# Where two groups of weight splits, a reciprocal of row sums and a gate's inverse stand in the order of an attention layer's first two groups

## Chip, core and metric

The kernel runs on one core of one Trainium2 chip. The time is the device time of one launch in microseconds (us); the engines are TensorE (PE in the profile, its weight loads PEld), VectorE (DVE), ScalarE (ACT), GpSimd (POOL) and SyncE's queue of transfers (SPq).

## What is computed

The input x has 4 batches of 512 tokens with 1024 features. Each batch goes through one attention block and one gate:

```python
xn = layernorm(x)
q, k, v = xn @ Wq.T, xn @ Wk.T, xn @ Wv.T        # 32 query heads, 8 key/value heads of 128
q, k = rmsnorm(q) * q_norm_w, rmsnorm(k) * k_norm_w
attn = softmax(q k.T / sqrt(128) + slope[head] * (key - query), causal)
s = (attn @ v) @ Wo.T
g = silu(xn @ W.T + bias + lora(xn))
out = x + s * g
```

Everything is float32. A product of two float32 operands is made from three passes on TensorE: each operand is split into a high part (rounded to the type fp32r, on ScalarE) and a low part (the operand minus its high part, on GpSimd for weights, on VectorE for activations), and hi*hi, lo*hi and hi*lo are summed.

## The kernel before

**Groups, steps and products.** There are 32 groups n (4 batches times 8 key/value heads), each with 4 steps j (one query head each), so 128 steps m = 4n + j. A step computes scores, softmax and attention of one head, and beside it a part of the next group's projection. The projection of a group (queries, keys, values and gate columns: 896 columns) is done with a 2 by 2 block scheme with seven products P1 to P7 in place of eight. Each product needs a combination of blocks of the weights, so for each group and each half h of its rows the kernel makes four sums of weight blocks (`weight_sum` and `weight_sums`, the instructions at L1390, L1392, L1395 and L1398 on VectorE for the first groups, L1132, L1133, L1135 and L1137 on GpSimd from group 2 on). The products of group n+1 are made by step: j = 0 makes P1 and P2, j = 1 makes P6 and P7, j = 2 makes P4, j = 3 makes P5 and P3. There are four slots for halves of split weights (`wh`, `wl`), so splits run one product ahead of the matmuls.

**How weights come.** In the first batch each half of a group's weights passes through one place in SBUF (`xtok` from group 2 on): SyncE loads it (`load_weights` L327, `load_gate_weights` L336 and L338), stores three raw blocks (`store_halves` L347 and L348), GpSimd sums the blocks in place, SyncE stores the four sums (`store_sums` L355), and only when that store has landed does the load of the next half begin. The split weights are read back from DRAM (`load_w` L302, 448 KB for a half). The halves follow one another in this order: (1,0), (1,1), (2,0), (2,1), (3,0), (3,1) and so on, (group, half). (2,0) is loaded in step 0, stored and summed around step 1, (2,1) is loaded at the end of step 2 and summed in step 3, and (3,0) is loaded in step 4 and summed in step 5. The load of (2,0) waits for GpSimd's first low half of P7 (L445, `sp.wait_ge(w_ready, ...)`). Group 1's P1, P2, P6 and P7 aren't read back: `split_later` (L802) splits them from where the load has put them.

**Order on each queue.** Every engine runs its own program in the order that is written out in its `step(n, j)`; engines meet at semaphores only.

- ScalarE (L979 to L1052): the four exponentials of the step (`exps`, L879), the high part of the attention output before (`head_out`, L891), high parts of the turned keys or queries, the scaling of the probabilities by the inverse row sums (`normalise`, L886), the gate's input (j = 0) or the output weights' high part (`split_b`, L822, after a wait for their load), the squares for the norms, the high parts of the turned probabilities of key tiles 0 to 2 (`probs_hi`, L858), the split of the first product of the list (`split_product`, L788; by j: P6, P4, P3, P1), `probs_hi` of key tile 3, the split of the second product (P7, P5, none, P2).
- VectorE: the four score tiles with bias and row maximum (`score_max`, L1319), `row_sums_inverse` (L1325), the low part of the attention output (L1330), low parts of turned queries or keys (L1284), the norms' factors and scaled rows (L1262 to L1274), the additions of the products to `raw` (L1314), the gate, the additions to `acc` (L1342 and L1344), and the low parts of turned probabilities (`probs_lo`, L1284). In step 0 it also makes group 1's eight weight sums: the first ahead of the inverse of the row sums, the others after the low part of the queries.
- GpSimd: the bias of the next step (L1100), the low part of the output weights (L1092), the low part of v (j = 0, L1105), low parts of weights (L1074, L1081) and the weight sums. In group 0 the sums of (2,0) and (2,1) stand at the end of steps 1 and 3, behind the low parts of that step's second product (P5 and P2). From group 1 on they stand ahead of the low parts.
- TensorE: scores of the step with the attention products of the step before between them, turned queries or keys, the pieces of the products, two output projections, the transposes of the probabilities of key tiles 0 to 2, an output projection, the transpose of key tile 3, an output projection. Three banks take the transposes in turn, so the transpose of key tile 3 waits for `probs_lo` of key tile 0, and the next step's third score tile waits for the maximum of its first.

**The gate.** `gate_sum` (L1348) adds one, `gate_inverse` (L1354) takes four reciprocals of 128 columns each, `gate_product` (L1360) ends it in step j = 1. The inverses stand at the end of step j = 0, but in the last group of a batch (`late_gate`) they are spread over the four pieces of j = 1.

Of the kernel before, what the change touches and what calls it, by code (L numbers as in the profile page):

```python
# [34 lines left out]
P1, P2, P6, P7, P4, P5, P3 = range(NP)  # L35
# [29 lines left out]
def ln_group(b):  # L65

    return 6 if b == 1 else 5
# [48 lines left out]
def u_count(n, p, t):  # L116
    return HW * n + 2 * p + t + 1
# [10 lines left out]
def build_layer(nc, x_tok, x_first, xT, wa, wo, wT, lora_a, lora_bt, lw, ffn_b, qw, kw, rel, slopes,  # L128
                ident, outT):
    with ExitStack() as ctx:  # L130
# [114 lines left out]
        def prep_tile(g, h, a, c):  # L245

            at = 2 * a + c
            return prep_place(g, h)[:, at * 896:at * 896 + 896].rearrange("p (k n) -> p k n", k=2)
# [507 lines left out]
        def _(act):  # L756
# [33 lines left out]
            def split_later(p, h):  # L790

                w = LATER + 2 * p + h
                at = w - 4
                if p in (P1, P2):
                    act.wait_ge(prep_in[h], 192 * 2 - 64)
                else:
                    act.wait_ge(prep_t[h], 4 + 3)
                if h == 0:
                    act.wait_ge(w_half, at // 2 + 1)
                else:  # L800
                    act.wait_ge(u_done, u_count(0, at // 2, 1))
                act.activation(wh[:, w % 4], prep_tile(1, h, *QUARTER[p]), ACT.Copy).then_inc(w_hi_done, 1)  # L802
# [11 lines left out]
            def split_product(n, p):  # L814
                for h in range(2):
                    split_w(HW * n + 2 * p + h)
# [54 lines left out]
            def probs_hi(m, k):  # L871
                w = slice(PT_AT[k], PT_AT[k] + S - P * k)
                take_hi(("p", m, k), pT_hi[:, w], slice(P * k, S))
# [35 lines left out]
            def ln_scale(b, t):  # L909
                act.wait_ge(ln_newton, 5 * (b + 1))  # L910
                act.activation(xtok[:, t, :], xtok[:, t, :], ACT.Identity, bias=shift_x[:, t:t + 1],
                               scale=rinv_x[:, t:t + 1]).then_inc(ln_ready, 1)
# [59 lines left out]
            for t in range(2):  # L972
                square_rows(0, P3, t)
            rsqrt(0, 1)
            split_later(P1, 1)
            for h in range(2):
                split_later(P2, h)

            def step(n, j):  # L979
                b, g = divmod(n, HKV)  # L980
                m, v = 4 * n + j, 4 * n + j - 2
                exps(m)
                last = n + 1 == NG
                if m > 0:
                    head_out(m - 1)
                if last:
                    normalise(m)
                if j == 0:
                    queries_hi(n, 1)
                if j == 1:  # L990
                    queries_hi(n, 2)
                    queries_hi(n, 3)
                if j == 3 and not last:
                    keys_hi(n + 1)
                    queries_hi(n + 1, 0)
                if not last:
                    normalise(m)
                if j == 0:
                    gate_in(n)
                elif not last:  # L1000
                    split_b(v + 1)
                pieces, fills = unit_pieces(n, j), x_fills(n, j)
                for u in pieces:
                    if u[1] in (P1, P2):
                        take_piece(*u)
                    elif u[1] in (P4, P5, P3):
                        square_rows(*u)
                    if fills:
                        x_hi(fills.pop(0))
                    if (g, j) == (6, 3) and b == 0 and u[1] == P3:  # L1010
                        ln_scale(1, 2 + u[2])
                    if u[1:] == (P1, 1):
                        gate_exp_of(n)
                        split_b(v + 1)
                    if u[1:] == (P2, 0):
                        values_hi(n)
                if j == 0 and last:
                    gate_exp_of(n)
                    values_hi(n)
                if n + 1 < NG:  # L1020
                    if j == 0:
                        for t in range(2):
                            square_rows(n + 1, P2, t)
                    if j == 2:
                        rsqrt(n + 1, 0)
                    if j == 3:
                        rsqrt(n + 1, 1)
                while fills:
                    x_hi(fills.pop(0))
                if (g, j) == (6, 1) and 0 < b < BATCH - 1:  # L1030
                    for t in range(NT):
                        ln_scale(b + 1, t)
                for k in range(3):
                    probs_hi(m, k)
                if (g, j) == (ln_group(b + 1), 1) and b + 1 < BATCH:
                    ln_rsqrt(b + 1)
                if (g, j) == (6, 2) and b == 0:
                    ln_scale(1, 0)
                    ln_scale(1, 1)
                if m == 0:  # L1040
                    for h in range(2):
                        split_later(P6, h)
                else:
                    split_product(*[(n + 1, P6), (n + 1, P4), (n + 1, P3), (n + 2, P1)][j])
                if last:
                    split_b(v + 1)
                probs_hi(m, 3)
                if m == 0:
                    for h in range(2):
                        split_later(P7, h)  # L1050
                elif j != 2:
                    split_product(*[(n + 1, P7), (n + 1, P5), None, (n + 2, P2)][j])  # L1052

            for n in range(NG):
                for j in range(G):
# [162 lines left out]
        def _(dve):  # L1218
# [178 lines left out]
                    dve.wait_ge(prep_t[h], 4 * g + 3)  # L1397
                    dve.tensor_tensor(b21, b21, b22, ALU.subtract).then_inc(prep_t[h], 1)  # L1398

            def weight_sums(g, h):  # L1400
                for p in (P5, P7, P6, P4):
                    weight_sum(g, h, p)

            def low_first_half(p, h):
                w = 2 * p + h
                dve.wait_ge(w_hi_done, w + 1)
# [75 lines left out]
            def step(n, j):  # L1482
                b, g = divmod(n, HKV)
                m, v = 4 * n + j, 4 * n + j - 2
                more, next_x = n + 1 < NG, b + 1 < BATCH
# [6 lines left out]
                    scale_rows("q0")  # L1492
                score_max(m, 2)
                score_max(m, 3)
                if n == 0 and j == 0:
                    weight_sum(1, 0, P5)
                row_sums_inverse(m)
                if m > 0:
                    head_out(m - 1)
                if j == 0 and more:  # L1500
                    queries_lo(n, 1)
                    if n == 0:
                        weight_sum(1, 0, P7)
                        weight_sum(1, 0, P6)
                if j == 1 and more:
                    queries_lo(n, 2)
                    queries_lo(n, 3)
# [3 lines left out]
                if j == 0:  # L1511
                    row_factors(n, 1)
                    scale_rows("q2")
                    scale_rows("q3")
                    if n == 0:
                        weight_sum(1, 0, P4)
                        weight_sums(1, 1)
                if not more:
                    last_part(n, j)
                    return  # L1520
                late_gate = g == 7 and next_x
                pieces, fills = unit_pieces(n, j), x_fills(n, j)
                turned = []
                for i, u in enumerate(pieces):
                    p, t = u[1:]
# [127 lines left out]
```

## Time and profile before

| | us |
|---|---|
| median of 3 runs | 2654.61 (2654.4 to 2656.84) |
| the profiled execution, its own time | 2655.72 |
| its span | 2653.9 |
| TensorE busy | 2583.1 (97%) |
| VectorE, ScalarE, GpSimd busy | 1699.8, 1764.6, 1718.0 |
| mean granted TensorE clock | 0.995 of full speed |

The span is the stretch from the first to the last instruction. Busy time is the time in which an engine has an instruction running; for TensorE ends are modelled, so that two matmuls that follow each other overlap a little in the rows. A row of the timeline gives the start, the duration, the engine, the line of the kernel, the operation and the tiles, and in brackets how long the engine had been idle before it and whose result it had waited for.

### The profile page before, as it was taken

To read this page: it belongs to the slowest core of one execution; us is meant where nothing else is said; L and a number is where in the kernel's file an instruction comes from. 1 tells how busy PE (TensorE), PEld (TensorE's weight loads), DVE (VectorE), ACT (ScalarE), POOL (GpSimd) and SP (SyncE) were. 2 spreads that over 40 slices of the span, in tenths; PEclk is the share of its full clock that TensorE was granted. 3 is DMA by queue.
4 is the path that set the end of the run, shared out by engine and by line. 5 is a ranking of instruction groups with operands and counts; after the bars stand their busy time and mean duration, and the time that the engine had idled before them with its cause. 6 is when DMAs were issued, how large, how long until landed. Compare 5 with 4: busy or idle time off the path is not lost.

```text
span 2653.9 us, 39893 instructions
## 1 busy us (share of the span) xinstructions
PE 2583.1 (97%) x13840; PEld 2288.9 (86%) x13840; DVE 1699.8 (64%) x3533; ACT 1764.6 (66%) x4633; POOL 1718.0 (65%) x839
## 2 busy tenths in 40 slices
PE   6789999999999999999999999999999999999997
PEld 5778888888888888888888888888888888888886
DVE  7565656666766665666667666666666756656656
ACT  4565666767767666667766667666777666667764
POOL 3577887785767565655667756565666766656555
PEclk9899999999999999999999999999999999999999
DMA  7868878875354333433344433433334533333323
GB/s 283 289 219 278 265 261 272 271 258 166 118 171 154 113 106 118 140 112 118 106 137 155 128 119 111 144 106 118 109 104 137 189 106 108 115 116 112 112 78 131
DMA packets 171896, 414.78 MB, mean 156 GB/s; under 512 B 31024, under 2 KB 63920, under 8 KB 170800
## 3 DMA queue, kind: packets, MB, share of 16 engines
q1 hardware_dynamic: 170144, 410.19, 47.1%
q8 instruction: 112, 1.84, 0.3%
q10 hardware_dynamic: 1552, 2.04, 0.2%
q14 instruction: 88, 0.72, 0.1%
HBM read 339.81 MB, written 89.13 MB: 162 GB/s over the span
## 4 chain that ended last, share of the span: by engine, by line
PE 90%; DVE 3%; DMA 2%; POOL 2%; ACT 1%; SPq 1%; issue 0%; ACTq 0%; POOLq 0%; DVEq 0%
PE proj L508 21%; PE proj L510 21%; PE proj L509 21%; PE tr L608 5%; PE tr L588 3%; PE sc L508 3%; PE sc L509 3%; PE sc L510 3%; PE ot L509 3%; PE ot L510 3%; PE ot L508 3%; DMA wu<-xtok 1%; PE tr L581 1%; DMA wl<-wu 1%; POOL wl L1081 1%
## 5 line engine op out<-in xcount | busy, mean ns | idle before, releaser
L1081 POOL TENSOR_TENSOR wl<-wl,wh 128x896 fp32r<-128x896 f32 x428 | 909.1, 2156 | 552.3 <-ACT wh L788 552.2
L508 PE MATMUL proj<-wh,xh 128*128 128x448 f32 x1792 | 670.7, 374 | 7.3 <-ACT raw L827 2.2
L509 PE MATMUL proj<-wl,xh 128*128 128x448 f32 x1792 | 657.9, 367 | 0.0
L510 PE MATMUL proj<-wh,xl 128*128 128x448 f32 x1792 | 657.8, 367 | 0.0
L1092 POOL TENSOR_TENSOR wb_lo<-wb_lo,wb_hi 128x1024 fp32r<-128x1024 f32 x128 | 307.7, 2404 | 303.7 <-ACT wb_hi L822 303.7
L879 ACT ACTIVATE misc<-misc,negmax 128x128 f32<-128x128 f32 (+3 forms) x512 | 286.7, 565 | 266.3 <-DVE negmax L1319 266.1
L508 PE MATMUL proj<-o_hi,wb_hi 128*128 128x512 f32 x1024 | 425.2, 415 | 7.4 <-DVE acc L1344 3.5
L1344 DVE TENSOR_TENSOR acc<-acc,proj 128x512 f32<-128x512 f32 x476 | 324.8, 683 | 149.7 <-PE proj L510 147.8
L858 ACT ACTIVATE pT_hi<-tr 128x512 fp32r<-128x512 f32 (+3 forms) x512 | 197.5, 440 | 325.9 <-PE tr L608 325.9
L510 PE MATMUL proj<-o_hi,wb_lo 128*128 128x512 f32 x1024 | 403.6, 394 | 0.0
L509 PE MATMUL proj<-o_lo,wb_hi 128*128 128x512 f32 x1024 | 401.3, 392 | 0.0
L788 ACT ACTIVATE wh<-wl 128x896 fp32r<-128x896 f32 x428 | 387.9, 965 | 19.7 <-DMA wl<-wu 19.2
L1314 DVE TENSOR_TENSOR raw<-raw,proj 128x448 f32<-128x448 f32 x320 | 197.4, 617 | 301.9 <-PE proj L510 300.1
L508 PEld LDWEIGHTS proj<-wh,xh 128*128 128x128 f32 x1792 | 337.9, 189 | 37.1 <-ACT raw L827 4.9
L510 PEld LDWEIGHTS proj<-wh,xl 128*128 128x128 f32 x1792 | 337.4, 188 | 30.0
L509 PEld LDWEIGHTS proj<-wl,xh 128*128 128x128 f32 x1792 | 338.1, 189 | 27.8
L1319 DVE CUSTOM_DVE_ANT_0 misc<-sc,misc 128x128 f32<-128x128 f32 (+3 forms) x512 | 240.9, 487 | 175.9 <-PE sc L510 174.7
L1284 DVE TENSOR_TENSOR pT_lo<-tr,pT_hi 128x512 fp32r<-128x512 f32 (+3 forms) x512 | 226.6, 484 | 74.7 <-ACT pT_hi L858 74.4
L834 ACT ACTIVATE junk<-raw 128x128 f32<-128x128 f32 x640 | 189.8, 301 | 97.2 <-DVE raw L1314 93.4
L886 ACT ACTIVATE misc<-misc,rs_inv 128x128 f32<-128x128 f32 (+3 forms) x512 | 245.2, 558 | 1.0 <-DVE rs_inv L1325 1.0
L508 PEld LDWEIGHTS proj<-o_hi,wb_hi 128*128 128x128 f32 x1024 | 193.4, 189 | 51.7 <-DVE acc L1344 4.1
L1100 POOL TENSOR_SCALAR misc<-misc,slope 128x512 f32<-128x512 f32 x128 | 233.6, 1825 | 4.1 <-DMA misc<-rel 4.1
(135 smaller groups left out, 4438.1 us busy)
## 6 DMA issues: line engine op xcount, KB each, us to landing
wl<-wu SPq DMA_DIRECT2D x426, 448.0 KB, 3.9
wb_lo<-wo_in SPq DMA_DIRECT2D x128, 512.0 KB, 3.3
wu<-xtok SPq DMA_DIRECT2D x13, 1792.0 KB, 9.7
wo_in<-wo SPq DMA_DIRECT2D x32, 512.0 KB, 6.2
xtok<-wa SPq DMA_DIRECT2D x52, 256.0 KB, 4.0
wu<-xtok SPq DMA_DIRECT2D x13, 896.0 KB, 6.2
gate_dram<-misc SPq DMA_DIRECT2D x32, 256.0 KB, 5.0
xtok<-xT SPq DMA_DIRECT2D x28, 256.0 KB, 5.1
```

Of the source, the lines that this page charges most:

```text
L508: pe.matmul(out, hi_l, hi_r, start=first, stop=False, skip_group_check=onto)
L509: pe.matmul(out, hi_l, lo_r, start=False, stop=False, skip_group_check=onto)
L510: return pe.matmul(out, lo_l, hi_r, start=False, stop=last, skip_group_check=onto)
L788: act.activation(w_slot(wh, w), w_slot(wl, w, True), ACT.Copy).then_inc(w_hi_done, 1)
L879: act.activation(p, p, ACT.Exp, bias=negmax[:, i:i + 1], scale=-1.0, accum_out=rowsum[:, i:i + 1]).then_inc(exp_done, 1)
L886: ins = act.activation(p, p, ACT.Copy, scale=rs_inv[:, i:i + 1])
L1081: pool.tensor_tensor(w_slot(wl, w), w_slot(wl, w, True), w_slot(wh, w), ALU.subtract).then_inc(w_ready, 1)
L1092: pool.tensor_tensor(wb_lo[:, v % 2, :], wb_lo[:, v % 2, :].bitcast(F32), wb_hi[:, v % 2, :], ALU.subtract).then_inc(wb_ready, 1)
L1100: pool.tensor_scalar(bias_sb[:, m % 2, :], rel_sb[:], slope[:, m % H:m % H + 1], None, ALU.mult).then_inc(bias_ready, 1)
L1284: dve.tensor_tensor(dst, bank, hi, ALU.subtract).then_inc(tr_free, 1)
L1319: dve.tensor_tensor_reduce(prob[:, P_AT[i]:P_AT[i] + w], sc_ps[i % 2][:, 0:w], bias_sb[:, m % 2, S - w:S], -1.0, 3e38, ALU.add, ALU.min, n ...
L1344: dve.tensor_tensor(a, a, bank, ALU.add).then_inc(out_free, 1)
```

## The change

On ScalarE the rest of group 1's early splits (P1's second half and P2) goes from ahead of step 0 to behind its exponentials. In steps 1, 3, 4 and 5 the split of the second product is taken out of its place at the end of the step and stands behind the exponentials of the next step, ahead of `head_out`. In the first two groups `probs_hi` of key tile 3 stands directly behind those of key tiles 0 to 2, ahead of the first product's split. On VectorE the inverse of step 0's row sums has no weight sum ahead of it any more, six of group 1's eight weight sums stand together behind the low part of the queries, and the last two behind the scaled rows. The gate's inverses of group 0 move from the end of step 0 to step 1. GpSimd's and SyncE's programs aren't changed.

```diff
@@ scalar, before and in step(n, j)
             rsqrt(0, 1)
-            split_later(P1, 1)
-            for h in range(2):
-                split_later(P2, h)
+
+            def second(n, j):
+
+                split_product(*[(n + 1, P7), (n + 1, P5), None, (n + 2, P2)][j])
+
+            def deferred(n, j):
+
+                return 0 < 4 * n + j < 6 and j != 2
 
             def step(n, j):
...
                 exps(m)
                 last = n + 1 == NG
+                if m == 0:
+                    split_later(P1, 1)
+                    for h in range(2):
+                        split_later(P2, h)
+                elif deferred(*divmod(m - 1, 4)):
+                    second(*divmod(m - 1, 4))
                 if m > 0:
                     head_out(m - 1)
...
+                if n < 2:
+                    probs_hi(m, 3)
                 if m == 0:
                     for h in range(2):
                         split_later(P6, h)
...
-                probs_hi(m, 3)
+                if n >= 2:
+                    probs_hi(m, 3)
                 if m == 0:
                     for h in range(2):
                         split_later(P7, h)
-                elif j != 2:
-                    split_product(*[(n + 1, P7), (n + 1, P5), None, (n + 2, P2)][j])
+                elif j != 2 and not deferred(n, j):
+                    second(n, j)
@@ vector, step(n, j)
                 score_max(m, 3)
-                if n == 0 and j == 0:
-                    weight_sum(1, 0, P5)
                 row_sums_inverse(m)
                 if m > 0:
                     head_out(m - 1)
                 if j == 0 and more:
                     queries_lo(n, 1)
                     if n == 0:
-                        weight_sum(1, 0, P7)
-                        weight_sum(1, 0, P6)
+                        for h in range(2):
+                            for p in (P5, P7, P6):
+                                weight_sum(1, h, p)
...
                     if n == 0:
-                        weight_sum(1, 0, P4)
-                        weight_sums(1, 1)
+                        for h in range(2):
+                            weight_sum(1, h, P4)
...
-                late_gate = g == 7 and next_x
+                late_gate = g == 7 and next_x or n == 0
```

## Rows read from the trace of the kernel before

**Rows 1.** Page, part 1: busy time, share of the span, instructions by engine.

```profile
PE 2583.1 (97%) x13840; PEld 2288.9 (86%) x13840; DVE 1699.8 (64%) x3533; ACT 1764.6 (66%) x4633; POOL 1718.0 (65%) x839
```

**Rows 2.** Waits of TensorE, 86 to 420 us: for whom, total us, times, longest.

```profile
PE tr L608 <- DVE pT_lo L1284: 11.3, 4, 6.0
PE sc L508 <- DVE negmax L1319: 6.2, 4, 2.8
...
PE proj L508 <- DVE acc L1344: 1.5, 1, 1.5
```

**Rows 3.** Two stretches: busy time of each engine, granted clock, transfers' share, GB/s.

```profile
112.00:116.00 4.00, 2.21 (x9) 2.12 (x10) 3.38 (x9) 1.70 (x3) 3.79 (x3) 0.50 1.02 417
...
330.00:400.00 70.00, 70.00 (x372) 62.25 (x371) 41.88 (x86) 48.46 (x130) 57.70 (x28) 1.00 0.80 266
```

**Rows 4.** Timeline of TensorE, steps 0 to 6: start, us, what, idle before and releaser.

```profile
113.79 0.48 PE L608 MATMUL tr<-ident_sb,misc 128*128 128x128 f32 x1 [6.02 <-DVE pT_lo L1284]
...
135.21 0.44 PE L508 MATMUL sc<-kT_hi,qT_hi 128*128 128x384 f32 x1 [0.74 <-DVE negmax L1319]
...
152.98 0.47 PE L608 MATMUL tr<-ident_sb,misc 128*128 128x128 f32 x1 [3.59 <-DVE pT_lo L1284]
...
180.09 0.44 PE L508 MATMUL sc<-kT_hi,qT_hi 128*128 128x384 f32 x1 [1.07 <-DVE negmax L1319]
...
206.37 0.44 PE L508 MATMUL sc<-kT_hi,qT_hi 128*128 128x384 f32 x1 [2.81 <-DVE negmax L1319]
...
233.81 0.47 PE L508 MATMUL proj<-wh,xh 128*128 128x448 f32 x1 [0.53 <-POOL wl L1081]
```

**Rows 5.** Timeline of VectorE, steps 0 and 4.

```profile
94.14 2.85 DVE L1390 TENSOR_TENSOR xtok<-xtok 128x896 f32<-128x896 f32 x1 [3.98 <-DMA wu<-xtok]
...
109.80 3.39 DVE L1354 RECIPROCAL misc<-misc 128x128 f32<-128x128 f32 x4
113.11 1.80 DVE L1284 TENSOR_TENSOR pT_lo<-tr,pT_hi 128x512 fp32r<-128x512 f32 x4
...
182.66 0.69 DVE L1319 CUSTOM_DVE_ANT_0 misc<-sc,misc 128x512 f32<-128x512 f32 x1 [1.01 <-PE sc L510]
```

**Rows 6.** Timeline of ScalarE, steps 0, 1, 3 and 4.

```profile
114.30 0.28 ACT L858 ACTIVATE pT_hi<-tr 128x128 fp32r<-128x128 f32 x1 [2.38 <-PE tr L608]
...
129.25 1.06 ACT L822 ACTIVATE wb_hi<-wb_lo 128x1024 fp32r<-128x1024 f32 x1 [4.56 <-DMA wb_lo<-wo_in]
...
181.69 0.95 ACT L788 ACTIVATE wh<-wl 128x896 fp32r<-128x896 f32 x1 [1.09 <-DMA wl<-wu]
...
184.03 0.70 ACT L879 ACTIVATE misc<-misc,negmax 128x512 f32<-128x512 f32 x1
```

**Rows 7.** Timeline of GpSimd, steps 0 and 5.

```profile
111.15 2.08 POOL L1074 TENSOR_TENSOR wl<-xtok,wh 128x896 fp32r<-128x896 f32 x1 [3.87 <-ACT wh L802]
...
115.50 2.11 POOL L1074 TENSOR_TENSOR wl<-xtok,wh 128x896 fp32r<-128x896 f32 x1 [0.21 <-ACT wh L802]
...
220.77 2.13 POOL L1132 TENSOR_TENSOR xtok<-xtok 128x896 f32<-128x896 f32 x1 [1.88 <-DMA wu<-xtok]
```

**Rows 8.** Timeline of SyncE's queue, steps 0 and 1.

```profile
104.17 0.37 SPq L355 DMA_DIRECT2D wu<-xtok  x1
...
109.46 0.37 SPq L355 DMA_DIRECT2D wu<-acc  x1
117.69 3.96 SPq L327 DMA_DIRECT2D xtok<-wa  x8
```

**Rows 9.** The chain of waits, 130 to 234 us: start, us, what held it.

```profile
151.60 5.95 DMA wu<-xtok
...
178.83 6.26 POOL wl L1081 x3
185.09 2.10 POOL xtok L1132
...
194.12 6.84 DMA wu<-xtok
...
229.57 4.20 POOL wl L1081 x2
```

More of the change, by code:

```diff
@@ L1398, in weight_sum @@
                     dve.tensor_tensor(b21, b21, b22, ALU.subtract).then_inc(prep_t[h], 1)
-            def weight_sums(g, h):
-                for p in (P5, P7, P6, P4):
-                    weight_sum(g, h, p)
             def low_first_half(p, h):
```

## The prediction

> **What bounds the kernel.** I began with the busy times: TensorE has 97% of the span [rows 1], so only what gives TensorE a wait, or takes one away, can move the end. Next I asked whom TensorE waits for from the start of step 0 on. The waits that the change can touch are behind the low parts of probabilities, the row maxima and the output additions, some 19 us in nine waits [rows 2]. A later stretch shows TensorE busy for 70.00 of 70.00 us at full clock [rows 3], so past step 7 nothing that another engine does earlier is worth anything. All that can be won lies in steps 0 to 6, and a lead or a delay that TensorE has at the end of step 6 is carried to the end of the kernel unchanged. The waits stand in order in [rows 4]. After a long wait the granted clock is at its lower level: in the 4 us that hold the wait of 6.02 it was 0.50 [rows 3], 1.2 instead of 2.4 GHz, though TensorE had run at 2.4 before it idled.
>
> The last view is the chain of waits [rows 9]. It says that the small waits hang on one ring: load a half's weights, store them, sum them on GpSimd, store the sums (151.60 and 194.12), load the next half. It ends in step 6, where GpSimd makes both low parts of P4 from 229.57 on, right behind the sums of (3,0), and TensorE takes up the second half at 233.81 [rows 4]. So at 233.81 the ring, not TensorE, sets the time. That is the point on which I settle the sum.
>
> **Step 0.** VectorE's work from 94.14 to 113.11 is nearly unbroken: the sums, with the inverse of the row sums between them, then the gate's four reciprocals, 109.80 to 113.11 [rows 5]. The order of the sums costs nothing in itself, since they are all still there; the inverse of the row sums comes some 6 us earlier, ScalarE scales the probabilities before TensorE needs them, and TensorE's P2 pieces start about 2 us earlier. But the transpose of key tile 3 waits for VectorE. Without the reciprocals `probs_lo` starts at 109.8, and the transpose runs at 110.4 instead of 113.79 [rows 4]: 3.4 us won. The idle time before it stays near 6 us, because what TensorE did earlier it also ends earlier; the slow clock stays.
>
> The reciprocals go to step 1, one behind each piece: 3.39 / 4 = 0.85 us each [rows 5]. A piece's 12 matmuls last some 2.3 us at 70.00 / 372 = 0.19 us from start to start [rows 3], more than an addition and a reciprocal, so three are hidden; the fourth would hold `probs_lo` back by 0.4 us, and that is covered by ScalarE's wait below. Cost nothing; without that cover 0.4.
>
> **What that does to the ring.** ScalarE used to split P6 at once and take key tile 3 at 114.30 [rows 6]. Now key tile 3 comes first, at 110.9, and P6's splits behind it. The first takes 0.95 us (the duration of a split, [rows 6]), so GpSimd starts P6 at 112.05 instead of 111.15 [rows 7]. Its low half takes 2.1 us, three of them end P7's first half at 118.35, against 115.50 + 2.11 = 117.6. SyncE waits for exactly that before it loads (2,0), at 117.69 [rows 8]: the ring starts 0.7 us late. The high part of the output weights waits for a load behind it on the same queue (4.56 us of waiting, until 129.25 [rows 6]), and now until 129.95. ScalarE has that wait ahead of the high parts of step 1's probabilities. Of TensorE's 3.4 us some 0.3 are left at the end of step 1.
>
> A second thing happens in the queue. Group 1's last sums now stand side by side, so the store of (1,0), issued at 104.17, goes out at about 108.3, and the store of (1,1) at about 109.5 as before [rows 8]. Its cost for the load at 118.4 is bounded by 0 (both landed) and by one more store less the gap, worked out under the second rival as 2.6. I take 0.3 of it, nearer the lower end, since the load's eight parts are issued over 3.96 us [rows 8] and a backlog shrinks meanwhile.
>
> **Steps 2 and 3.** Key tile 3's high part no longer stands behind a split: the wait of 0.74 goes. P5's split, which waited for its load ahead of the exponentials, now waits behind them; the attention output and the squares come up to 2 us earlier, and the wait of 3.59 starts and ends with them [rows 4]. TensorE is about 1.9 us ahead at the start of step 3. There ScalarE waits for the next output weights, whose load hangs on the ring (from 151.60 on, [rows 9]) and comes 0.4 to 1.0 later. The lead shrinks to between 0.3 and 0.9; I take 0.5.
>
> **Step 4, where the ring loses.** The wait of 1.07 goes [rows 4]. The last score's maximum was taken at 182.66 and took 0.69 [rows 5]; now it is ready at 183.35 - 1.07 - 0.5 = 181.8. The last exponential takes 0.70 [rows 6] and ends at 182.5. Before, P2's second half was split at 181.69, when its load had come, ahead of the exponentials [rows 6]. Now both halves of P2 stand behind them. GpSimd can take up the first at 182.5 + 0.95 = 183.45, and needs 2 x 2.1 us. Behind them on its queue stand the sums of (2,1), which used to start at 185.09, right when P1's and P2's last three low parts ended (178.83 + 6.26, [rows 9]). Now they start at 187.7: **2.6 us later**. That is the price of the deferral, and it is paid on the ring: the store goes out at 196.7 instead of 194.12, its landing frees the place for (3,0) [rows 9], and the sums of (3,0), which waited 1.88 us for their data at 220.77 [rows 7], start at 223.4.
>
> **Steps 5 and 6.** The wait of 2.81 and its slow clock go [rows 4], because key tile 3 is no longer behind P6's splits. TensorE then waits some 2 us for the low parts of P6 and P7, whose loads are 2.6 late. It is at P4 at about 230, near 2 us early. But P4's low halves end at 229.57 + 2.1 + 2.6 = 234.3 and 236.4. Idle for over 4 us, TensorE comes back at 1.2 GHz, as after 6.02 [rows 3, 4]. The first half's six matmuls fill the 2.1 us until the second is there even so; if another 1.3 us are slow, they cost 0.7. The bounds for the clock are 0 (no fall, as after 0.53) and 2 (half of a 4 us stretch). The other deferred splits (P7 in step 5, P5 in step 6) are covered: GpSimd is still at P6 and at the sums when they come.
>
> **Sum.** 2.6 for the ring and 0.7 for the clock, less nothing: all that steps 0 to 5 win is waited away at P4. 2655.7 + 3.3 = 2659.0 for the profiled execution. It lies 1.1 above the median, so 2657.9 for the median. With the lead into step 4 between 0.3 and 0.9 and the clock between 0 and 2 the likeliest case alone spans 2656.8 to 2659.8.
>
> **Rivals.**
> - *The ring doesn't lose.* If the exponentials of step 4 end by 181.7, P2's splits are bound by their load, as before, and GpSimd's sums start on time. That needs a lead of 1.3 us into step 4. Then the ring is 0 to 1 late, and P4 comes when it came before: 2654.6 to 2656. For it: the lead was 1.9 a step before. Against it: the output weights' load in step 3. Chance 0.22.
> - *Stacked stores, slower.* The two stores of group 1 go out 1.2 us apart. One store of four sums takes 5.95 to 6.84 us to land [rows 9]. If the second moves only behind the first, it lands at 109.5 + 2 x 5.95 = 121.4, and the load issued at 118.4 moves about 2.6 us later than it could. Then the ring is 3.3 late from the start, TensorE is 2.1 late instead of 0.5 early in step 4, and the sums of (2,1) start 5.2 late; with the clock's 0.7 that is 5.9, 2660.5. It decides once the load of (2,0) is held over 2 us. Against it: the eight parts of the load are paced by their issue. Chance 0.13. The Trainium skill, "DMA: Bandwidth & Descriptors", section "Queues, rings and completion order", says that on each transfer engine descriptors are consumed in ring order, which speaks for this rival; by that rule the time would be 2660.5, and no row here shows two such stores side by side.
> - *The ring has slack that I don't see, faster.* If ScalarE's waits for loads in steps 1 and 3 moved with TensorE, the 3.4 of step 0, 0.74, 1.07 and 2.81 + 1.7 of clock would all count: 9.7 us, 2644.9. Against it: rows 9 show the ring without a gap. Chance 0.10.
> - The change does what it says: each moved instruction has its place in the diff, and no wait is taken off a semaphore.
>
> **Numbers.** The forecast has 0.55. A measurement of this kernel tells 0.2%, 5.3 us, from no change, that is 2649.3 and 2659.9. Faster: the last rival, 0.10. Slower: the second rival, 0.13, and 0.05 of the forecast's upper end. Same: 0.72. The range takes in the forecast, the first rival and the second, and reaches down part of the way to the last: 2651.5 to 2661.
>
> **What would show it.** Right: no wait of 2.81 before step 5's third score; the reciprocals in step 1; SyncE's first load of (2,0) near 118.4; the sums of (2,1) starting near 187.7 behind P2's low parts; the sums of (3,0) near 223.4; TensorE waiting some 4 us for `wl` in step 6, at 1.2 GHz behind it, and no difference in pace past 250 us. Wrong: the sums of (2,1) at 185 or before, or TensorE waiting in step 6 for something else than GpSimd.

## The result and the profile after

The changed kernel takes 2660.02 us (median of 15 runs, 2655.92 to 2663.26), the kernel before 2654.68 in the same sittings. The ratio is 1.0020, with a 95% interval of 1.0011 to 1.0028: **slower by 5.3 us**, clear of the scatter and right at the 0.2% that the prediction took as its bound (2659.9). One of the 15 runs of the kernel before took 3630.14 us, where the others took 2652.71 to 2656.84, and isn't in the ratio. The forecast was 2657.9 with a range of 2651.5 to 2661.

The profiled execution took 2660.54 us, its span is 2658.7 (4.8 more than before). Step 0 begins 0.9 us earlier in this trace than in that of before (its third score tile starts at 86.21 in place of 87.12); that lies in the start of the run, ahead of anything the change touches. Shifts of places in the trace are therefore told below as read and, in brackets, with those 0.9 us taken out.

The waits of TensorE in the changed kernel, 86 to 420 us (for whom, total us, times, longest), against [rows 2]:

```profile
PE tr L608 <- DVE pT_lo L1298: 13.2, 4, 4.9
PE proj L508 <- DVE acc L1358: 4.4, 1, 4.4
...
PE tr L588 <- DVE raw L1288: 2.7, 2, 1.8
PE sc L508 <- DVE negmax L1333: 2.3, 2, 1.6
```

The waits for the row maxima fell from 6.2 to 2.3 us, as they were meant to. Those for the low parts of probabilities grew from 11.3 to 13.2, and two others that had been short are long: the one for an addition to `acc` grew from 1.5 to 4.4, those for scaled rows from 0.4 to 2.7.

The same places as [rows 4] in TensorE's timeline:

```profile
108.70 0.48 PE L608 MATMUL tr<-ident_sb,misc 128*128 128x128 f32 x1 [4.90 <-DVE pT_lo L1298]
...
150.61 0.33 PE L608 MATMUL tr<-ident_sb,misc 128*128 128x128 f32 x1 [3.77 <-DVE pT_lo L1298]
...
160.24 0.65 PE L588 MATMUL tr<-ident_sb,raw 128*128 128x128 f32 x4 [1.83 <-DVE raw L1288]
...
202.96 0.80 PE L508 MATMUL proj<-o_hi,wb_hi 128*128 128x512 f32 x1 [4.43 <-DVE acc L1358]
...
237.17 0.47 PE L508 MATMUL proj<-wh,xh 128*128 128x448 f32 x1 [0.53 <-POOL wl L1095]
```

Key tile 3 of step 0 is turned at 108.70 instead of 113.79 (4.2 us earlier without the start). The waits of 0.74, 1.07 and 2.81 are gone. TensorE waits in step 3 (1.83 at 160.24, where it had waited 0.35) and in step 4 (4.43 at 202.96, where it had waited 1.48) instead, and takes up the second half of P4 at 237.17 instead of 233.81, 3.4 us late (4.3).

Two stretches of the changed kernel (busy time of each engine, granted clock, transfers' share, GB/s), against [rows 3]:

```profile
160.00:164.00 4.00, 3.76 (x14) 3.44 (x15) 2.81 (x9) 3.31 (x9) 1.61 (x1) 0.65 0.93 270
...
204.00:208.00 4.00, 4.00 (x11) 3.06 (x10) 1.78 (x5) 1.21 (x3) 0.67 (x1) 0.50 0.87 316
...
330.00:400.00 70.00, 70.00 (x377) 62.42 (x376) 43.78 (x92) 46.55 (x121) 57.78 (x29) 1.00 0.80 263
```

Behind both longer waits the granted clock is at its lower level, 1.2 GHz, for part or all of 4 us, though it had been 1.00, 2.4 GHz, from 156 to 160 and from 196 to 200. From 330 to 400 us TensorE is busy throughout at full clock, as before.

GpSimd around the sums, against [rows 7] and [rows 9]:

```profile
178.81 4.21 POOL L1095 TENSOR_TENSOR wl<-wl,wh 128x896 fp32r<-128x896 f32 x2 [6.01 <-ACT wh L788]
185.09 4.19 POOL L1095 TENSOR_TENSOR wl<-wl,wh 128x896 fp32r<-128x896 f32 x2 [2.07 <-ACT wh L788]
189.24 2.12 POOL L1146 TENSOR_TENSOR xtok<-xtok 128x896 f32<-128x896 f32 x1
...
224.15 2.12 POOL L1146 TENSOR_TENSOR xtok<-xtok 128x896 f32<-128x896 f32 x1 [1.01 <-DMA wu<-xtok]
...
232.91 4.20 POOL L1095 TENSOR_TENSOR wl<-wl,wh 128x896 fp32r<-128x896 f32 x2
```

Here is the ring. GpSimd stands idle for 2.07 us between the low parts of P1 and P2, since ScalarE's split of P2 is behind the exponentials of step 4, and the sums of (2,1) start at 189.24 in place of 185.09, those of (3,0) at 224.15 in place of 220.77, the low parts of P4 at 232.91 in place of 229.57.

The chain of waits of the changed kernel, where [rows 9] had gone over the sums:

```profile
183.36 0.82 ACT misc L879 x2
184.18 0.27 ACT wh L788
...
184.92 0.94 ACT wh L788
185.86 0.49 ACT o_hi L891
186.37 0.69 DVE o_lo L1344
...
193.51 5.10 DVE raw L1288 x2
...
202.36 0.55 DVE acc L1358
202.96 0.80 PE proj L508
```

From P2's split (`wh`) it doesn't go on to GpSimd's low parts and sums, but over the attention output, VectorE's scaled rows and the gate to the addition that TensorE waits for in step 4. So P2's split delays two paths, this one and the ring. They meet in step 6: P4's first low part is ready at 235.01, TensorE takes it up at 235.19, and the second half waits for GpSimd.

### The profile page after: what moved, and what is told of

Read it like the earlier page. It is cut to its first block, busy times and chain, and to the rows that moved or that the text cites. A ratio compares the mean times of both kernels' runs of the same rounds, so it can differ in the third digit from the quotient of the medians.

```text
span 2658.7 us, 39893 instructions
## 1 busy us (share of the span) xinstructions
PE 2584.6 (97%) x13840; PEld 2290.3 (86%) x13840; DVE 1706.4 (64%) x3533; ACT 1764.2 (66%) x4633; POOL 1716.2 (65%) x839
## 3 DMA queue, kind: packets, MB, share of 16 engines
q10 hardware_dynamic: 1552, 2.04, 0.2%
## 4 chain that ended last, share of the span: by engine, by line
PE 89%; DVE 4%; ACT 2%; POOL 2%; DMA 1%; issue 1%; SPq 1%; ACTq 0%; POOLq 0%; DVEq 0%
PE proj L508 21%; PE proj L510 21%; PE proj L509 21%; PE tr L608 5%; PE tr L588 3%; PE sc L508 3%; PE sc L509 3%; PE sc L510 3%; PE ot L509 3%; PE ot L510 3%; PE ot L508 3%; PE tr L581 1%; DVE raw L1288 0%; DMA wl<-wu 0%; DVE wl L1417 0%
```

## The experiments

Twelve kernels ran. Every ratio is against the kernel before in the same runs; 0.001 is 2.65 us.

The expectations name three explanations. *Ring theory*: the time is set by the ring of load, store, sums, store and next load, and a change costs what it delays there. *VectorE theory*: TensorE is held up in steps 3 and 4 by VectorE, whose scaling runs beside GpSimd's instructions. *Slack theory*: the ring has time to spare, and TensorE's own waits are what counts.

### One part at a time: which engine's edits cost?

ScalarE's edits alone. Against the changed kernel, all of VectorE's edits are undone:

```diff
                 score_max(m, 3)
+                if n == 0 and j == 0:
+                    weight_sum(1, 0, P5)
                 row_sums_inverse(m)
...
-                        for h in range(2):
-                            for p in (P5, P7, P6):
-                                weight_sum(1, h, p)
+                        weight_sum(1, 0, P7)
+                        weight_sum(1, 0, P6)
...
-                        for h in range(2):
-                            weight_sum(1, h, P4)
+                        weight_sum(1, 0, P4)
+                        weight_sums(1, 1)
...
-                late_gate = g == 7 and next_x or n == 0
+                late_gate = g == 7 and next_x
```

> Only ScalarE's edits of the change; VectorE's program is the one of before. Ring theory: the loss is ScalarE's, so it is here whole: 2659 to 2661, and the 3.4 us of step 0 aren't even won. VectorE theory: steps 3 and 4 run as in the changed kernel whenever ScalarE's step 2 ends early, so 2658 to 2661 too; the two differ by the next run.

2663.88 us, ratio 1.0033 (1.0020 to 1.0045): 9 us slower than before, 4 slower than the whole change.

VectorE's edits alone. They are the part of the change's diff that stands above under "vector"; ScalarE's program is the one of before, so no split is put off and key tile 3 stands where it stood. Its last line:

```diff
-                late_gate = g == 7 and next_x
+                late_gate = g == 7 and next_x or n == 0
```

> Only VectorE's edits; ScalarE's program is the one of before. Ring theory: the transpose of key tile 3 in step 0 comes 3.4 us earlier, P6's splits aren't held back by it, the ring starts no later than before, and nothing puts P2's split off: 2653 to 2655, no difference or up to 2 faster. VectorE theory: a lead into step 3 only lengthens the blocked scaling, 2654 to 2656. A loss of over 3 us here would say that it comes from the gate's inverse or the bunched stores.

2654.30 us, ratio 0.9998 (0.9989 to 1.0007): no difference. TensorE's transpose of key tile 3 in step 0 is earlier, at 111.91, and nothing comes of it.

So the loss is ScalarE's, VectorE's edits take back 4 us of it and give nothing by themselves. The two effects don't add, as the ring theory says of step 0: with VectorE late, key tile 3 (turned at 115.30 in the first of these runs) holds back P6's splits and with them the load of (2,0), which is issued at 123.34 there and at 116.74 in the changed kernel. The first run lies 3 us above what was expected of it: I hadn't counted that VectorE's edits are what makes the early key tile 3 bearable.

### The single part that the prediction blamed

P2's split of group 2, alone, on the kernel before:

```diff
                 exps(m)
+                if m == 4:
+                    split_product(2, P2)
...
-                elif j != 2:
+                elif j != 2 and m != 3:
                     split_product(*[(n + 1, P7), (n + 1, P5), None, (n + 2, P2)][j])
```

> The kernel before, with one single part of the change: P2 of group 2 is split behind step 4's exponentials. Ring theory: key tile 3's high part of step 3 isn't moved, so step 4 starts as before with its wait of 1.07, the exponentials end near 183.5 to 184, P2's low parts come 3 to 4 us later than before, and so do the sums of (2,1); the time is 2657 to 2659. Rival, many small parts: since putting P2 back in the full change won only 0.7 us, P2's place is worth under 1 us here too, 2654.5 to 2655.5.

2658.92 us, ratio 1.0015 (1.0007 to 1.0024): 4.4 us slower, as much as most of the change. GpSimd's timeline of this kernel:

```profile
174.80 4.28 POOL L1083 TENSOR_TENSOR wl<-wl,wh 128x896 fp32r<-128x896 f32 x2 [4.14 <-ACT wh L788]
183.27 4.20 POOL L1083 TENSOR_TENSOR wl<-wl,wh 128x896 fp32r<-128x896 f32 x2 [4.19 <-ACT wh L788]
187.42 2.13 POOL L1134 TENSOR_TENSOR xtok<-xtok 128x896 f32<-128x896 f32 x1
```

One moved split makes a hole of 4.19 us in front of P2's low parts and the sums. It also lengthens the wait of TensorE in step 4 from 1.5 us to the same 4.4 as in the changed kernel:

```profile
PE tr L608 <- DVE pT_lo L1286: 12.8, 4, 7.6
PE sc L508 <- DVE negmax L1321: 4.4, 5, 1.5
PE proj L508 <- DVE acc L1346: 4.4, 1, 4.4
```

The split pushes the attention output and the queries' high part back on ScalarE, VectorE starts its factors and scaled rows later and does them beside GpSimd's sums, and the addition that TensorE waits for comes behind all of it. In the trace of before the first of the small instructions for the factors took 0.66 us and the two scalings 3.23, here they take 1.75 and 5.09. So P2's place costs on two ways at once, the ring and step 4 itself. The chain of waits goes over the ring in this run and over step 4 in the changed kernel; no run takes one of the two away and leaves the other.

### Putting parts back into the change

P2 of step 3 back at the end of its step:

```diff
-                return 0 < 4 * n + j < 6 and j != 2
+                return 0 < 4 * n + j < 6 and j not in (2, 3)
```

> The changed kernel, but the second half of the splits that step 3 puts off (P2 of group 2) stands at the end of step 3 again. Ring theory: the sums of (2,1) start right behind P2's low parts, which come when their load has landed (183 plus two low parts), near 186 in place of 189.2, the sums of (3,0) 3 us earlier than in the changed kernel, and 2.5 to 4 us of the loss come back: 2656 to 2657.5. Rival, VectorE theory: VectorE, held up by GpSimd in steps 3 and 4, is what TensorE waits for (1.83 and 4.43 us); then the split's place is worth under 1 us: 2659 to 2660.5.

2659.37 us, ratio 1.0014 (1.0005 to 1.0023). The profiled execution does what the ring theory says, the sums of (2,1) start at 186.13 and those of (3,0) at 221.01, and it took 2657.48 us; but the median over 11 runs is 0.7 us below the change's only (1.6 by the two ratios, whose intervals overlap). The expectation of 2.5 to 4 us failed. TensorE comes to P4 ahead of GpSimd in this trace and waits 2.04 us for the first low part, which it doesn't in the changed kernel.

No split put off at all:

```diff
-                return 0 < 4 * n + j < 6 and j != 2
+                return False
```

> The changed kernel with no split put off at all, only the early high part of key tile 3 and VectorE's edits left. Ring theory: as with P2 alone put back, 2656 to 2657.5, since the other splits that are put off are covered, but with up to 2 us more, because P5's and P6's neighbours hold the exponentials back again (0.7 at step 2, 2 at step 5). VectorE theory: 2659 to 2661.

2657.75 us, ratio 1.0011 (1.0002 to 1.0020): 2.3 us below the change, 2.9 above before. VectorE's edits alone took 2654.30, so what is left of ScalarE's edits here, the early key tile 3 and group 1's first splits, costs 3.4 us by the medians, though the two intervals overlap. The splits put off aren't the whole loss.

Key tile 3 of step 0 behind P6's splits again:

```diff
-                if n < 2:
+                if n < 2 and m > 0:
                     probs_hi(m, 3)
...
-                if n >= 2:
+                if n >= 2 or m == 0:
                     probs_hi(m, 3)
```

> The changed kernel, with key tile 3's high part of step 0 behind P6's splits again (one place of eight). Ring theory, first part: P6's low parts start about 2 us earlier, the load of (2,0) comes 0.7 to 2 us earlier after the start of step 0, and 0.5 to 2 us come back: 2658 to 2659.5. Rival: the ring's start has slack or is given back by step 2, since P5's split waits for the exponentials: 2660.

2659.56 us, ratio 1.0021 (1.0012 to 1.0029): nothing, alone.

Both put back:

```diff
-                return 0 < 4 * n + j < 6 and j != 2
+                return 0 < 4 * n + j < 6 and j not in (2, 3)
...
-                if n < 2:
+                if n < 2 and m > 0:
                     probs_hi(m, 3)
```

> Both places that the ring theory holds responsible are put back: P2's split of step 3 and key tile 3 of step 0. Everything else of the change stays. Ring theory: the sums of (2,1) and of (3,0) start no later than before, and the time is that of before or up to 2 us below it, 2652.5 to 2655. VectorE theory: steps 3 and 4 still wait for VectorE, 2657 to 2659.

2656.86 us, ratio 1.0008 (0.9999 to 1.0017): 3.2 us below the change. It lies between what the ring theory expected (up to 2655) and what the VectorE theory did (from 2657). Each alone gave 0.5 to 0.7, both together 3.2, and 2.3 are left, at the edge of what the runs tell from nothing. That the two help only together fits one ring with two places where it is held up, but no run shows why the first alone gives so little; with medians that differ by less than their intervals this stays open. In this trace, too, TensorE is at P4 too early:

```profile
231.46 0.44 PE L508 MATMUL proj<-wh,xh 128*128 128x448 f32 x1 [2.02 <-POOL wl L1095]
```

### Is it VectorE beside GpSimd?

The wait of 1.83 in step 3 was in no step of the prediction. VectorE's scaling of two rows takes 5.05 us there. The run holds GpSimd's low parts of P3 back until it is done:

```diff
                 else:
+                    if m == 2:
+                        pool.wait_ge(q_ready, 5)
                     low_product(*[(n + 1, P6), (n + 1, P4), (n + 1, P3), (n + 2, P1)][j])
```

> The changed kernel, with one wait added on GpSimd: in step 2 it begins P3's low parts only when VectorE has scaled the first queries of the next group in step 3. VectorE theory: the two scalings of step 3 took 5.05 us because GpSimd's low parts ran beside them; without that they take 1.3 to 1.6, TensorE's wait of 1.83 goes and step 3 ends 2 to 3 us earlier; if that is what makes the loss, 2657 to 2658. Ring theory: the ring's next sums of (2,1) start only with P2's low parts behind step 4's exponentials, so they come earlier by what step 4 starts earlier, up to 2.5 us, and the time falls by as much, 2657.5 to 2659; with the sums no earlier, no time is won.

2659.19 us, ratio 1.0018 (1.0009 to 1.0027). VectorE's timeline at that place, in the changed kernel:

```profile
155.13 5.05 DVE L1288 SCALAR_TENSOR_TENSOR raw<-raw,tmp 128x512 f32<-128x512 f32 x2
```

and in this one, the same two instructions:

```profile
157.05 1.29 DVE L1290 SCALAR_TENSOR_TENSOR raw<-raw,tmp 128x512 f32<-128x512 f32 x2
```

Both are as expected of contention: 5.05 us beside GpSimd, 1.29 without. TensorE's wait of 1.83 and the slow clock behind it are gone, step 3 lasts 22.1 us (155.21 to 177.32) instead of 25.6 (153.17 to 178.81). But step 3 also begins 2.0 us later, so 1.5 of the 3.5 us are left at the start of step 4. The sums of (2,1) start 1.5 us earlier than in the changed kernel (187.77), those of (3,0) 1.6, and the span is 1.7 shorter; the median falls by 0.8, to 0.2 above the ring theory's range. P2 stands where it stood, and the wait of 4.43 in step 4 is in this trace too. VectorE's hold-up in step 3 is real and makes at most a small part of the loss. The same hold-up in step 4, where the scalings take 5.09 us here too, no run takes away.

### Moving the ring by itself

The strongest test leaves ScalarE as before and moves only GpSimd's sums (VectorE has its edits, which cost and bring nothing):

```diff
                 else:
+                    if m == 3:
+                        weight_sums(2, 1, (0,))        # the first two sums
                     low_product(*[(n + 1, P6), (n + 1, P4), (n + 1, P3), (n + 2, P1)][j])
+                if m == 1:
+                    weight_sums(2, 0)
...
-                if j in (1, 3) and n == 0:
-                    weight_sums(2, j // 2)
+                if m == 3:
+                    weight_sums(2, 1, (1,))            # the last two sums
```

> ScalarE as before, VectorE's edits of the change, and GpSimd reordered: the sums of (2,0) ahead of P5's low parts, and the first two sums of (2,1) ahead of P1's. The ring is made earlier where the change made it later. Ring theory: the store of (2,0)'s sums goes out 4 us earlier, that of (2,1) 3 to 5 us earlier, TensorE's waits in steps 5 and 6 (2.8, its slow clock 1.7, and 0.5) go, 2648 to 2651. If the ring isn't what sets the time, no difference, 2654 to 2656.

**2648.42 us, ratio 0.9978 (0.9969 to 0.9987): 6.2 us faster than before and 11.6 faster than the change.** It beats both kernels. Its GpSimd timeline:

```profile
136.68 2.10 POOL L1133 TENSOR_TENSOR xtok<-xtok 128x896 f32<-128x896 f32 x1
...
170.09 2.12 POOL L1133 TENSOR_TENSOR xtok<-xtok 128x896 f32<-128x896 f32 x1 [1.05 <-DMA wu<-xtok]
172.17 2.12 POOL L1134 TENSOR_TENSOR xtok<-xtok 128x896 f32<-128x896 f32 x1
174.90 8.38 POOL L1081 TENSOR_TENSOR wl<-wl,wh 128x896 fp32r<-128x896 f32 x4 [0.61 <-ACT wh L788]
183.23 2.13 POOL L1138 TENSOR_TENSOR xtok<-xtok 128x896 f32<-128x896 f32 x1
```

The sums of (2,0) start at 136.68 (before: 143.11, ahead of P5's low parts now), two sums of (2,1) fill time in which GpSimd had been idle, and the last two end at 187.6, 6.5 us before their end before. Of TensorE's waits the 1.5 us for an addition to `acc` in step 4 are gone, and none for a row maximum is longer than 1.8 us (2.8 before):

```profile
PE tr L608 <- DVE pT_lo L1291: 10.9, 4, 6.8
PE sc L508 <- DVE negmax L1326: 5.7, 4, 1.8
```

Then the same GpSimd order under the full change:

> The full change, with GpSimd's sums early as in the run that beat both kernels. Ring theory: the last two sums of (2,1) still stand behind P2's low parts, which the change puts off, so the loss against the kernel with early sums stays: 5 to 8 us above it, 2653 to 2656; against the change alone 4 to 6 us come back. Rival, slack: with the ring early the change's earlier exponentials count, and it is as good as the kernel with early sums, 2646 to 2649.

2655.75 us, ratio 1.0001 (0.9992 to 1.0010). The change costs 7.3 us more than the same order without it. The first two sums start at 168.84, but P2's low parts at 183.81 and the last sum ends at 192.3, not at 187.6: the deferral takes 4.7 of the ring's lead, as the ring theory said, and the slack theory failed.

With P2 of step 3 and key tile 3 of step 0 put back, and the sums early:

> The change with P2's split of step 3 and key tile 3's of step 0 put back, and GpSimd's sums early. Ring theory: the ring is as early as with the sums alone, and the splits put off in steps 1, 4 and 5 and the early key tile 3 have nothing left to cost: 2646.5 to 2649.5. Rival: those parts cost the 2 us that the change with both put back still lost: 2650 to 2651.

2650.42 us, ratio 0.9987 (0.9978 to 0.9996): 5.3 us of those 7.3 come back. Between the kernel with early sums and this one 2 us are left in the medians, as the rival said and 0.9 outside what the ring theory allowed; the two intervals overlap.

And with no split put off, only key tile 3 early in steps 1 to 7:

```diff
-                return 0 < 4 * n + j < 6 and j != 2
+                return False
...
-                if n < 2:
+                if 0 < m < 8:
                     probs_hi(m, 3)
```

> Sums early, no split put off in steps 1 to 5, key tile 3's high part early in steps 1 to 7 but not in step 0, VectorE's edits kept. It asks which of the two, the splits put off or key tile 3's place, costs or brings anything once the ring is early. The waits of 1.17 and 1.35 for the maxima in steps 5 and 6 should go: 2646 to 2648.5. If the early key tile 3 itself costs, because the first product's split behind it comes too late, 2649 to 2651.

2651.29 us, ratio 0.9986 (0.9977 to 0.9995). The early key tile 3 brings nothing even here: the time is 0.3 above what was expected if its place costs, and the plain order with early sums has a median 2.9 us lower, though the two intervals overlap.

### One number through all runs

In every profiled execution I took the span's end less the start of the first sum of (3,0):

| kernel | sums of (3,0) start | span | span less start |
|---|---|---|---|
| before | 220.77 | 2653.9 | 2433.1 |
| changed | 224.15 | 2658.7 | 2434.6 |
| P2 back | 221.01 | 2655.7 | 2434.7 |
| none put off | 222.85 | 2657.5 | 2434.7 |
| ScalarE only | 229.24 | 2663.6 | 2434.4 |
| VectorE only | 219.88 | 2653.5 | 2433.6 |
| P3's low parts held | 222.56 | 2657.0 | 2434.4 |
| key tile 3 back | 224.95 | 2660.6 | 2435.7 |
| both back | 220.37 | 2655.1 | 2434.7 |
| P2 alone | 223.28 | 2656.8 | 2433.5 |
| sums early | 214.33 | 2647.2 | 2432.9 |
| change, sums early | 218.62 | 2652.5 | 2433.9 |
| both back, sums early | 214.16 | 2648.6 | 2434.4 |
| key tile 3, sums early | 214.07 | 2648.4 | 2434.3 |

The starts differ by 15.2 us, the rest by 2.8. Where the ring stands at the sums of (3,0) the end of the kernel stands about 2434 us later. That alone doesn't show a cause, since whatever delays TensorE before may delay the ring as well. P4 shows more. In all 14 traces TensorE takes up its second half 13.0 to 13.1 us after that start, behind a wait of 0.27 to 0.54 us for GpSimd's low part, and in six of them it has waited 2.0 us for the first low part too. So at P4 the ring holds TensorE in every kernel, and a lead that TensorE brings there is lost. What is left in the rest divides the kernels too: without the early key tile 3 it is 2432.9 to 2433.6, with it 2433.9 to 2435.7.

## Why the prediction was right, and where it wasn't

It forecast no clear difference with a loss of 3.3 us; 5.3 were measured, inside the range, and at the edge of what the prediction counted as no difference.

**The step that carried the forecast held.** P2's split behind step 4's exponentials holds up the sums of (2,1), and through them everything to P4 in step 6. The run with this part alone lost 4.4 us, and moving the sums, with VectorE's edits that do nothing alone, gained 6.2. P4's second half was forecast to wait for the ring, and it does, 13.0 us behind the first of the sums of (3,0), as before. But the forecast isn't the whole of it. P2's split has a second path, over VectorE in step 4, that the forecast didn't have; that it reached P4 only 0.2 us behind GpSimd is luck for the forecast. And with no split put off 2.9 us of loss were left, of which the forecast had at most the 1 us that it left to the ring in its first rival.

**Step 0 held in kind.** 3.4 us forecast for key tile 3, 4.2 read. The load of (2,0) was forecast 0.7 late; it came 0.05 us early without the start's 0.9.

**Mis-sized: the lead into step 4.** "The lead shrinks to between 0.3 and 0.9; I take 0.5." At the start of step 3 TensorE was 2.6 us early (1.7; forecast 1.9), at the start of step 4 it was 1.3 late (2.2). The step that failed is step 3: I let only the output weights' load take from the lead, and left out that VectorE's scaling meets GpSimd's low parts of P3. In the trace of before TensorE waited 0.35 us there, too little for a row in [rows 4]. An earlier step 3 puts the scaling under more of GpSimd's two low parts, 5.05 us in place of 3.31, TensorE waits 1.83, and its clock falls, to 0.65 over 160 to 164. Step 3 lasted 25.6 us, 3.9 more than before and 3.5 more than with the low parts held back. With the 1.3 us late that were read in place of 0.5 early, the term for the ring, 2.6, becomes 4.4; 4.2 was read.

**Wrong: where TensorE would wait.** I forecast some 4 us of idle time in step 6 for P4's low parts, at 1.2 GHz behind it. It is a wait of 0.53 there, as before. The idle time is in step 4 instead, 4.43 us for an addition to `acc`, with the slow clock behind it (204 to 208). I had written that "all that steps 0 to 5 win is waited away at P4"; in fact P2's split also delays ScalarE's head output, so that VectorE starts its low part 1.0 us later (186.37 in place of 185.35), and the factors and scaled rows behind it then meet more of GpSimd's sums: the first small instruction took 1.74 us in place of 0.66, the two scalings 5.10 in place of 3.23. Together that is the 4.0 us by which the addition to `acc` is late (202.28 in place of 198.32). TensorE and GpSimd arrive at P4 together, both late. TensorE does bring a lead to P4 and wait it away, 2.0 us long, in six of the other traces, but not in the changed kernel. Nor is there the forecast wait of 2 us in step 5 for the low parts of P6 and P7.

**The rivals.** *The ring doesn't lose* is out: the sums started 4.2 us late. *The ring has slack* is out: 1.07, 0.74 and 2.81 us of waits went and the time rose. The argument against it was read too strongly, though: the chain of [rows 9] isn't without a gap, between 206.37 and 229.57 it goes over TensorE, ScalarE and VectorE. *Stacked stores*: the stores of group 1 did go out side by side, at 106.73 and 107.73, and the load of (2,0) was issued at 116.74 and its store of raw blocks at 126.43, 9.7 us later, where before it took 10.3 (117.69 to 128.03). So the stacked stores held nothing up. The time came near that rival's 2660.5 by another way. Two of the forecast's sums are off by 0.4: the rival's load is held 121.4 less 118.4, 3.0 and not 2.6 us, and the likeliest case reaches to 2654.6 + 2.8 + 2, 2659.4 and not 2659.8. Neither changes a chance. SyncE's queue in the changed kernel, against [rows 8]:

```profile
106.73 0.37 SPq L355 DMA_DIRECT2D wu<-xtok  x1
...
107.73 1.30 SPq L355 DMA_DIRECT2D wu<-acc  x1
116.74 4.00 SPq L327 DMA_DIRECT2D xtok<-wa  x8
```

What the Trainium skill says under "DMA: Bandwidth & Descriptors", "Queues, rings and completion order", that descriptors are consumed in ring order, may well hold; the trace agrees with it no further than that a load issued 9 us behind two such stores wasn't late.

**Beyond the ring.** The changed kernel has 1.4 us more between the sums of (3,0) and the end. Two waits there are longer: one of 1.42 at 247.59 (0.79 before), and one of 0.85 for scaled rows in step 7, at 254.39, where there was none. The second goes with the early key tile 3: it is in all ten traces that have it in step 7, 0.85 to 0.89 us long, and in none of the four without. In the kernel with both places put back it is

```profile
250.60 0.66 PE L588 MATMUL tr<-ident_sb,raw 128*128 128x128 f32 x4 [0.88 <-DVE raw L1288]
```

Key tile 3's place in step 7, ahead of the first product's split, was costed at nothing. The mechanism wasn't tried apart.

## What to carry to other kernels

An instruction moved "behind the critical ones" on one engine is ahead of everything that queues behind its consumer on another: ask what stands behind the low part on GpSimd's queue, not only who reads the weights. Waits that an engine shows at the end of a step can be slack of a longer ring through transfers; removing them pays only if the ring gets shorter. Here the places of two halves' sums in the ring were worth 6.2 us, and the waits that the change removed brought nothing. Where a lead is won, look at what it will now run beside.

## What I hadn't expected of the hardware

VectorE's two scalings of 128x512, with two inputs in SBUF, took 5.05 us beside GpSimd's instructions and 1.29 with GpSimd held back, 3.9 times as long; in step 4 they took 5.10 and small ones of 128x8 1.7 to 2.1 us each. One of step 4's, in the changed kernel:

```profile
189.34 2.04 DVE L1278 SCALAR_TENSOR_TENSOR tmp<-ss,tmp 128x8 f32<-128x8 f32 x1
```

That is about as long as the sum of GpSimd that starts 0.1 us before it (189.24, 2.12 us), for eight columns, as if the small instruction waited for the whole one of GpSimd; one of the same kind with 12 columns took 0.17 at 325.67 in this trace, where GpSimd was idle. The Trainium skill says this in "SBUF — State Buffer", "Who interferes with whom": a VectorE instruction with two SBUF inputs contends with a GpSimd instruction that reads SBUF, and the shared ports are an exclusive lock. The trace agrees, with 2.04 us against 2.12. A cost of a VectorE instruction that is taken from one place of the trace doesn't hold where GpSimd is busy in another way.
